# Second attention layer of a four-layer model on one core: where the output bias is added, when the normalised rows are turned, and how VectorE's row work is cut

## The reference, cut to what matters

```python
q = (query @ Wq + bq).reshape(b, sq, 16, 64)      # query = layernorm(x), without gain or bias
k = (ctx @ Wk + bk).reshape(b, 154, 16, 64)
v = (ctx @ Wv + bv).reshape(b, 154, 16, 64)
attn = softmax(einsum('bqhd,bkhd->bhqk', q, k) / 8)
out = einsum('bhqk,bkhd->bqhd', attn, v).reshape(b, sq, 1024)
out = out @ Wo + bo + residual                    # residual = query
y = layernorm(out) * ln_gamma + ln_beta
x = x + tanh(g_xattn[1]) * y
```

## Time and profile before

| what | us |
| --- | --- |
| median of 3 runs | 1551.88 (1550.76 to 1552.78) |
| the profiled execution, its own time | 1550.85 |
| its span in the profile | 1548.9 |
| of it, the 32 units of layer 1's attention, first exponential to last output bias product | 314.4 to 569.1 |
| PE busy over the whole span | 1357.6 (88%) |
| DVE, ACT, POOL busy | 944.2, 723.3, 529.6 |

### The profile page before, as it was taken

How to read it: one execution, slowest core, us unless ns; L and a number is a source line. 1 busy time by engine, 2 the same in 40 slices (tenths; PEclk the granted TensorE clock), 3 DMA queues, 4 the chain that set the end, 5 groups by cost and what they waited for, 6 DMA issues and landing times. The chain is left out here.

```text
span 1548.9 us, 25635 instructions
## 1 busy us (share of the span) xinstructions
PE 1357.6 (88%) x9124; PEld 767.6 (50%) x9124; DVE 944.2 (61%) x2135; ACT 723.3 (47%) x1950; POOL 529.6 (34%) x625
## 2 busy tenths in 40 slices
PE   5899779879989989987998889899987988998998
PEld 3544337545555646554433556565654444443443
DVE  6566621454656664267664888878774855665764
ACT  3355413466656434343443565656664243453222
POOL 2410340545333262342001474747552220001443
PEclk9799989999999999998999999999988997999999
DMA  2445120201000012322120000000000001000000
GB/s 62 138 131 131 42 68 26 44 7 15 1 1 1 1 38 72 95 67 55 35 52 1 1 1 1 1 1 1 2 1 0 1 14 20 10 2 1 7 7 14
DMA packets 66992, 45.31 MB, mean 29 GB/s; under 512 B 17564, under 2 KB 60261, under 8 KB 66869
## 3 DMA queue, kind: packets, MB, share of 16 engines
q1 hardware_dynamic: 61013, 34.48, 8.7%
q0 software_dynamic: 4096, 8.40, 2.1%
q10 hardware_dynamic: 1760, 0.82, 0.3%
HBM read 24.91 MB, written 13.89 MB: 25 GB/s over the span
## 5 line engine op out<-in xcount | busy, mean ns | idle before, releaser
L3464 ACT ACTIVATE L2a_pr<-psum,L2a_negmax 128x512 f32<-128x512 f32 (+3 forms) x256 | 132.0, 530 | 94.3 <-DVE L2a_negmax L3590 40.2
L573 ACT ACTIVATE L1x_praw<-psum,L1x_negmax 128x154 f32<-128x154 f32 x256 | 95.9, 391 | 81.4 <-DVE L1x_negmax L669 81.2
L318 POOL TENSOR_TENSOR L1x_pm<-L1x_praw,L1x_total 128x1024 f32<-128x1024 f32 x32 | 60.7, 1898 | 145.2 <-DVE L1x_total L675 90.4
L84 PE MATMUL psum<-ident 128*128 128x512 f32 x178 | 93.4, 664 | 16.3 <-PEq L3875 7.5
L3326 PE MATMUL psum<-ident,L2a_pr 128*128 128x128 f32 x640 | 85.9, 278 | 19.2 <-DVE L2a_pT L3603 11.9
L669 DVE TENSOR_REDUCE L1x_negmax<-psum 128x4 f32<-128x616 f32 x64 | 50.8, 795 | 57.7 <-PE psum L370 57.0
L3326 PEld LDWEIGHTS psum<-ident,L2a_pr 128*128 128x128 f32 x640 | 71.7, 142 | 25.0 <-issue 21.3
L2016 POOL TENSOR_TENSOR L3f_scaled<-L3f_sg,L3f_wide 128x512 f32<-128x512 f32 (+1 forms) x44 | 55.7, 1271 | 66.4 <-ACT L3f_sg L2097 43.9
L1649 DVE TENSOR_REDUCE L3x_negmax<-psum 128x6 f32<-128x924 f32 (+1 forms) x48 | 47.8, 1012 | 43.9 <-PE psum L1181 35.5
L3212 POOL TENSOR_TENSOR L2a_pr<-L2a_pr,L2a_total 128x768 f32<-128x768 f32 x32 | 48.7, 1520 | 69.9 <-DVE L2a_total L3619 69.6
L3209 POOL TENSOR_TENSOR L2a_pr<-L2a_pr,L2a_total 128x1024 f32<-128x1024 f32 x29 | 56.5, 1949 | 46.1 <-DVE L2a_total L3619 46.0
(11 more groups left out here) (745 smaller groups left out, 3423.1 us busy)
## 6 DMA issues: line engine op xcount, KB each, us to landing
expert_arena<-in_L_ffn_w SPq DMA_DIRECT2D x16, 256.0 KB, 4.4
group_in<-zero SPq DMA_DIRECT2D x2, 1472.0 KB, 9.6
L1f_xs<-group_in SPq DMA_DIRECT2D x10, 256.0 KB, 4.1
group_out<-L1f_ys SPq DMA_DIRECT2D x10, 256.0 KB, 2.3
L1f_gu<-in_L_ffn_gate_up_w SPq DMA_DIRECT2D x8, 256.0 KB, 3.3
slots_in<-zero SPq DMA_DIRECT2D x1, 1280.0 KB, 10.4
L0f_xs<-slots_in SPq DMA_DIRECT2D x5, 256.0 KB, 4.0
resid<-in_x SPq DMA_DIRECT2D x4, 256.0 KB, 5.7
```

Of the source, the lines that this page charges most:

```text
L84: self.nc.tensor.matmul(self.psum[:, bank, :].rearrange("p (t d) -> p t d", d=D), self.ident[:], self.ident[:].unsqueeze(1).to_broadcast([ ...
L318: nc.gpsimd.tensor_tensor(pm[:, n % 2].rearrange("p j t k -> p (j t) k"), praw[:, n % 3, :, :, 0:MAIN].rearrange("p j t k -> p (j t) k"), ...
L573: nc.scalar.activation(praw[:, n % 3, j, t, :], psum[:, 2 * u + j, x * CTX:(x + 1) * CTX], ACT.Exp, bias=negmax[:, n % 2, u, j, x:x + 1], ...
L3464: ins = nc.scalar.activation(pr[:, i % RING, SEQ * j + lo:SEQ * j + hi], psum[:, bank + j, lo:hi], ACT.Exp, bias=negmax[:, i % RING, e:e + ...
```

## The change: what it does

1. **Bias.** The L421 products go. Before the loop one product of ones with `bo` gives all 128 partitions the bias (`bob`), and GpSimd adds it to the normalised rows `xn` of the batch, in place, after its work on unit 2, 10, 18 and 26. `finished`'s first step waits for this (`biased`).
2. **Output between the turned tails and their copy.** TensorE's `output(n-5)` moves ahead of the two waits and of whatever stood in H1, right behind `tails`.
3. **Turned rows a unit ahead.** Batches 2 and 3 have their rows turned at the end of units 7 and 15 in bank H1, and not in units 8 and 16 in H0; `turned` of units 8 and 16 waits for ScalarE's copy of them (`xt`). In unit 0 ScalarE's copy of batch 1's turned rows goes between the two halves of the exponentials. `normed(2)` and `normed(3)` move to units 6 and 14.
4. **ScalarE's square roots.** `rows_root` moves to units 5 and 13, `root` stays at g = 6 (units 14, 22, 30); both now stand between `exps(n, 0)` and `exps(n, 1)`.
5. **VectorE's row work in parts.** `summed` is cut in three and `finished` in six; parts now stand between the copies of the turned weights and `maxima(n, 1)` (units 3, 11, 12, 14, 15, 16, 22, 23, 24, 30, 31, 32) or at the end of the body.

```diff
@@ gpsimd
+                    if n % NG == 2:
+                        f = n // NG
+                        pool.wait_ge(s["xt_ps"], f + 1)
+                        rows_b = xn[:, f % 3]
+                        nc.gpsimd.tensor_tensor(rows_b, rows_b, bob[:].unsqueeze(1).to_broadcast([P, QT, D]), ALU.add).then_inc(s["biased"], 1)
@@ tensor, output(m)
-                                                start=(g == 0 and t == 0), stop=False, skip_group_check=True)
-                    if g == NG - 1:
-                        if b == 0:
-                            pe.wait_ge(s["bo"], 1)
-                        for t in range(QT):
-                            last = nc.tensor.matmul(psum[:, OUT, t * P:(t + 1) * P], core.ones[0:1, :], bo[0:1, :],
-                                                    start=False, stop=True, skip_group_check=True)
+                                                start=(g == 0 and t == 0), stop=(g == NG - 1), skip_group_check=True)
@@ tensor, before the loop
+                    if i == 3:
+                        pe.wait_ge(s["bo"], 1)
+                        nc.tensor.matmul(psum[:, OUT, 0:D], core.ones[0:1, :], bo[0:1, :], start=True, stop=True).then_inc(s["bob_ps"], 1)
@@ tensor, the loop
+                            if b in (1, 2) and g == 0:
+                                pe.wait_ge(s["xt"], b + 2)
...
-                            if g == 0:
-                                rowsT(b + 1, H0)
+                            if n == 0:
+                                rowsT(1, H0)
                             query(n + NG, H0)
...
                     if n >= 3 and n % 2 and n - 2 < NS:
                         tails(n - 2)
+                    if 0 <= n - 5 < NS:
+                        output(n - 5)
                     if n < NS:
                         if n >= 2:
                             pe.wait_ge(s["pt"], 2 * (n - 2) + 2)
...
+                        if b < 2 and g == 7:
+                            rowsT(b + 2, H1)
...
-                    if 0 <= n - 5 < NS:
-                        output(n - 5)
@@ scalar, the loop
                         exps(n, 0)
+                        if n == 0:
+                            rowsT(1, H0)
+                        if n in (5, 13):
+                            rows_root(2 + n // NG)
+                        if g == 6 and b:
+                            root(b - 1)
                         exps(n, 1)
...
-                        if g == 0:
-                            rowsT(b + 1, H0)
                         query(n + NG, H0)
+                        if b < 2 and g == 7:
+                            rowsT(b + 2, H1)
...
-                    if n == 6:
-                        rows_root(2)
-                    if g == 6 and b:
-                        if b == 1:
-                            rows_root(3)
-                        root(b - 1)
@@ vector, before the loop
                     value(1, i, i)
+                    if i == 0:
+                        dve.wait_ge(s["bob_ps"], 1)
+                        nc.vector.tensor_copy(bob[:], psum[:, OUT, 0:D]).then_inc(s["bob"], 1)
@@ vector, the loop (behind turned(n - 2), ahead of maxima(n, 1))
+                    if n == 3:
+                        summed(2, 1)
+                    if n == 11:
+                        summed(3, 0)
+                    if n == 12:
+                        summed(3, 2)
+                    if b:
+                        if g in (6, 7):
+                            finished(b - 1, g - 5)
+                    if b >= 2 and g == 0:
+                        finished(b - 2, 4)
                     if n < NS:
                         maxima(n, 1)
@@ vector, the loop (end of the body)
+                    if n == 2:
+                        summed(2, 0)
+                    if n == 3:
+                        summed(2, 2)
+                    if n == 6:
+                        normed(2)
+                    if n == 11:
+                        summed(3, 1)
+                    if n == 14:
+                        normed(3)
                     if b and g == 5:
                         finished(b - 1, 0)
...
+                    if b and g == 7:
+                        finished(b - 1, 3)
                     if b >= 2 and g == 0:
-                        finished(b - 2, 2)
+                        finished(b - 2, 5)
```

More of the change, by code:

```diff
@@ L255, in wide_attention @@
         "bq", "pad", "vec", "xn", "xt_ps", "xt", "q_ps", "q", "k_ps", "k", "v_ps", "v", "v_act", "sc", "mx", "ex", "rs", "nm", "nt",
-        "tr", "pt", "tt_ps", "tt", "pv", "o", "op", "yr", "yvar", "ysd", "bo_ps", "bo", "rvar", "rsd", "summed")}
+        "tr", "pt", "tt_ps", "tt", "pv", "o", "op", "yr", "yvar", "ysd", "bo_ps", "bo", "rvar", "rsd", "summed", "bob_ps", "bob", "biased")}
     back = [nc.alloc_semaphore(f"{L}_back{b}") for b in range(B)]
@@ L629, in _, with summed @@
                 v = Steps(dve, s["vec"], 0, 0)
-                def summed(b):
-                    dve.wait_ge(back[b], 16 * 2 * QT)
-                    pairs = results[b].rearrange("p (k d) -> p k d", d=D)
-                    wt = core.slot_wt[:, b * QT:(b + 1) * QT, :].rearrange("p t r -> p (t r)")
-                    v.step(nc.vector.tensor_tensor(pairs, pairs, wt.unsqueeze(2).to_broadcast([P, 2 * QT, D]), ALU.mult))
-                    v.done()
-                    halves = results[b].rearrange("p (t r d) -> p t r d", r=2, d=D)
-                    nc.vector.tensor_tensor(y[:], halves[:, :, 0, :], halves[:, :, 1, :], ALU.add).then_inc(s["summed"], 1)
-                    dve.wait_ge(s["summed"], b + 1)
-                    update_rows(core, v, b, y[:].rearrange("p t d -> p (t d)"), slots_gate, y, parts, mv)
-                    nc.vector.tensor_scalar(core.std[:, b * QT:(b + 1) * QT], core.stat[:, b * QT:(b + 1) * QT, 1], LN_EPS, None, ALU.add).then_inc(s["rvar"], 1)
+                def summed(b, part):
+                    rows_b = y[:].rearrange("p t d -> p (t d)")
+                    if part == 0:
+                        dve.wait_ge(back[b], 16 * 2 * QT)
+                        pairs = results[b].rearrange("p (k d) -> p k d", d=D)
+                        wt = core.slot_wt[:, b * QT:(b + 1) * QT, :].rearrange("p t r -> p (t r)")
+                        v.step(nc.vector.tensor_tensor(pairs, pairs, wt.unsqueeze(2).to_broadcast([P, 2 * QT, D]), ALU.mult))
+                    if part == 1:
+                        v.done()
+                        halves = results[b].rearrange("p (t r d) -> p t r d", r=2, d=D)
+                        nc.vector.tensor_tensor(y[:], halves[:, :, 0, :], halves[:, :, 1, :], ALU.add).then_inc(s["summed"], 1)
+                        dve.wait_ge(s["summed"], b + 1)
+                        add_rows(core, v, b, rows_b, slots_gate, y)
+                    if part == 2:
+                        keep_rows(core, v, b, y, parts, mv)
+                        nc.vector.tensor_scalar(core.std[:, b * QT:(b + 1) * QT], core.stat[:, b * QT:(b + 1) * QT, 1], LN_EPS, None, ALU.add).then_inc(s["rvar"], 1)
                 def normed(b):
@@ L691, in finished @@
                         dve.wait_ge(s["op"], NG * (b + 1))
+                        dve.wait_ge(s["biased"], b + 1)
                         nc.vector.tensor_tensor(y[:], psum[:, OUT, :].rearrange("p (t d) -> p t d", d=D), xn[:, b % 3], ALU.add).then_inc(s["yr"], 1)
@@ L700, in finished @@
                         nc.vector.tensor_scalar(sdv[:], mv[:, :, 1], LN_EPS, None, ALU.add).then_inc(s["yvar"], 1)
-                    if part == 1:
+                    if part == 2:
                         dve.wait_ge(s["ysd"], b + 1)
@@ L706, in finished @@
                             v.step(nc.vector.tensor_scalar(y[:, t, :], y[:, t, :], mv[:, t, 0:1], sdv[:, t:t + 1], ALU.subtract, ALU.mult))
+                    if part == 3:
                         v.done()
@@ L721, in _ @@
                     value(1, i, i)
-                summed(0)
+                    if i == 0:
+                        dve.wait_ge(s["bob_ps"], 1)
+                        nc.vector.tensor_copy(bob[:], psum[:, OUT, 0:D]).then_inc(s["bob"], 1)
+                for part in range(3):
+                    summed(0, part)
                 normed(0)
-                summed(1)
+                for part in range(3):
+                    summed(1, part)
                 normed(1)
@@ L768, in _ @@
                             grouped.table(dve, v, 0)
-                finished(B - 1, 0)
-                finished(B - 1, 1)
-                finished(B - 1, 2)
+                for part in range(6):
+                    finished(B - 1, part)
 def add_rows(core, v, b, src, gate, new, base=None):
```

16 lines of the change are left out of this document (4 added, 12 removed).

## The result

The changed kernel takes 1541.64 us in the median of 12 runs (1536.02 to 1546.6), the kernel before, on the same chip, 1552.33 (1548.61 to 1562.0, 12 runs). The medians differ by 10.7 us. The ratio of the two kernels' runs is 0.9921, 95% interval 0.9905 to 0.9937: 12 us less, 10 to 15. The forecast was 1542.2, in the range 1536 to 1549, and faster at 0.86.

A forecast was written before the change was run, and what follows sets the result against it. The prediction took TensorE's own list to bound the middle of the stage. Gains of 17.3 us less losses of 7.7 gave 9.6: 1541.2 us for the profiled run, 1542.2 against the median, range 1536 to 1549.

The forecast's parts named there:

- Output ahead of the waits: TensorE's output product moved ahead of the copy waits: mostly 0.83 us a unit, unit 21 losing 0.6; 7.3 us won.
- Bias: Four bias products of 1.08 us leave TensorE's loop, 4.3 us, less 0.3 ahead of the loop: 4.0 us won.
- Turned rows: Rows turned a unit ahead: 3.17 us won in unit 16 and 1.3 in unit 8, 4.5 in all.
- First units: Units 0 to 5: earlier rows copy and spread sums put TensorE 1.0 us ahead in unit 5.
- Unit 12: Sums leave the front of the maxima, ending the projection's 0.4 us wait for turned copies: 0.5 us won.
- Square roots: ScalarE's roots between the exponentials' halves delay query copies in units 5, 14, 22 and sums in 30: 3.6 us lost.
- VectorE's parts: Row work ahead of the second maxima, slowed beside GpSimd's product, stalls units 11, 12, 15, 16, 23: 4.1 us lost.
- Rival A: Cover is better: TensorE never catches up with the late copies, losses vanish, 17.3 us won: 1534.6 us; 14%.
- Rival B: VectorE's parts pay for all three GpSimd products, and for its bias in unit 11: 4 us more, 1546 us; 13%.
- Rival C: No change: parts and roots cost what was won around them, or gaps reappear at the 1.47 waits: 1551 us; 9%.
- Rival D: Slower: new stalls halve TensorE's clock, 1.7 us a drop; six drops use up the 9.6, ten make 1559 us; 5%.
- a sign of being wrong: In TensorE's clock: a halved clock in stretches that were at 1.0 before would show the prediction wrong.

The follow-up runs named there:

- the fastest kernel: Changed kernel with square roots behind the query copies, sums in three parts behind the second maxima, OUT read a unit earlier; ratio to before 0.9824.
- the kernel with roots and parts back: Changed kernel with square roots behind the query copies and VectorE's row work whole behind the second maxima again; ratio to before 0.9913.
- the sums spread: Changed kernel with square roots behind the query copies and the row sums in three parts, each behind second maxima; ratio to before 0.9865.
- the two experiments: Kernel before with only the rows turned a unit ahead, ratio 0.9960; fastest kernel with rows turned in units 8 and 16 again, ratio to before 0.9899.
- the kernel with the roots back: Changed kernel with only ScalarE's square roots behind the query copies again, VectorE's parts still ahead of the second maxima; ratio to before 0.9899.
- OUT read earlier: Kernel with spread sums and square roots behind the query copies, OUT read in units 12, 20, 28, not 13, 21, 29; ratio to before 0.9824.

## Why the prediction was right

The time, the sign and the mechanism came out: gross gain against stalls behind late query copies. Its net for the stage was 9.9 (9.6 and the 0.3 ahead of the loop); measured are 12.4. That the median, 1541.6, lies only 0.6 from the forecast's 1542.2 is partly luck: by the ratio, the 1551.88 that it started from become 1539.6, which is 2.6 lower, about what the stage won beyond the forecast. Step by step:

- **Output ahead of the waits, 7.3.** From the starts of unit after unit in the traces, units 5, 7, 9, 11, 15, 17 and 19 win 1.05 to 1.07 each and not 0.83, 7.4 in all; units 23 and 27 win 0.8 and 0.9, unit 25 nothing; unit 21 loses 1.0, and 0.15, 0.4, 0.15, 0.14 and 0.76 come back as short waits in units 20, 18, 22, 24 and 26. With 0.3 at the end the sum is 6.8; the ninth wait of 0.83, in unit 31, wasn't in the forecast's list. Both the single gain and what is given back had been set too low.
- **Bias, 4.0.** 4.3 in the stage (shown by its removal from the fastest kernel), less 0.5 ahead of the loop. GpSimd's additions cost nothing, as said. Not seen: the products of unit 12 had been cover worth 1.25. It was cover for what VectorE's sums in one piece delay: the same 1.25 stands in the kernel with roots and parts back, and with the sums spread no turning behind unit 12 waits.
- **Turned rows, 4.5.** 3.7 to 4.9 in the two experiments; the waits of the earlier trace rows and of the earlier trace rows for `L1x_xnT` are gone.
- **First units, 1.0.** 2.2, with a scatter of 1 or more. The 3.64 of the earlier trace rows shrank to 2.16, as worked out, and unit 4's second scores come 2.1 earlier (1.9 was said). The forecast then let half of it be lost again by unit 5; it was not. (By its two rows `summed(2)` takes 4.7 us and not 4.8; no term hangs on that.)
- **Unit 12, 0.5.** 0.9, in the kernels where no part stands ahead of its maxima.
- **Square roots, 3.6.** 3.6 by undoing them. The places were less well met than their sum: unit 5 cost 1.3 (forecast 0.2, on the ground that its scores are late against the exponentials; in the trace they are late by 0.13 alone, 347.01 against 346.88; and the odd unit's list, 5.94 in the forecast, is 5.71), unit 14 1.6, of which 0.4 comes back in unit 15 and is lost again in unit 16, unit 22 0.1 to 0.5 (1.0), unit 30 0.7 (0.5), unit 13 nothing, as said.
- **VectorE's parts, 4.1.** 2.6 from unit 5 on, against pieces behind the maxima: 0.87 in unit 11, 1.15 in unit 12, 0.7 in units 14 to 16, 0.3 in 23 and 0.3 near the end, against 0.8 won back in unit 25, where TensorE then doesn't wait for the turned weights' copy. This is the term that was mis-sized, in units 11, 12 and 16 and by the gain that it had not.

So the losses were 6.2 and not 7.7, and the first units gave 1.2 more: with these two the stage's 9.9 becomes 12.6, against 12.4 measured. The errors of the output term (0.5 too high) and of unit 12 (0.4 too low) nearly cancel. Rival A (no losses) falls by the kernel with the roots back, and again by the one with the sums spread. Rival B falls: L644 was held by one product of GpSimd and not by three. Rival C would have needed losses of 17.3, where 6.2 were measured. Rival D: the halved clock takes 10.24 us of the stage, before and after; one stretch of 3.4 moved from 521 to 339 us, behind a pause of 1.59 in unit 4, and no stretch was added. This row (columns as in the result) is of a stretch that stood at 1.0 before. The prediction had named that as a sign of being wrong, but with 10.24 us of half clock in both it costs the stage nothing.

```profile
339.30:342.70 3.40, 3.40 (x19) 2.03 (x17) 2.65 (x5) 1.66 (x9) 2.54 (x3) 0.51 0.00 0
```

What none of the steps had: the row sums in one piece would have cost 1.43 + 1.25 us in unit 12 once output and bias were gone. The parts ahead of the maxima were better than that and worse than parts behind.

Two rules had been weighed. By the Trainium skill ("SBUF — State Buffer", "Who interferes with whom") the later of two such operations is blocked for the whole of the earlier. L644 began 0.91 before GpSimd's product ended; blocked fully it would take 0.91 + 1.22 = 2.13, and it took 1.98. The gated addition of unit 16, begun 0.90 before the end, took 1.45 where the rule gives 0.90 + 0.75 = 1.65. The trace nearly agrees: both are 0.15 to 0.2 us shorter. The forecast's start at 2.05 behind the unit's start gave an end of 3.27 where 3.13 was measured. By the Trainium skill ("ScalarE: Activation LUTs", "What ACT_TABLE_LOAD costs") each switch costs the load and as much again. Here the load is 1.28, what follows starts 0.02 later, and all roots together cost 3.6 and not 3.6 + 11.6. The advice in the Trainium skill ("ScalarE: Activation LUTs", "Table sets: the hidden batching unit") is to do all the exponentials together and then all the square roots. Here it is the place that counts: behind the query copy the same loads cost TensorE next to nothing (in the kernel with the roots back the turning behind unit 14 waits 0.19), between the halves they cost the 3.6.

## What to carry to other kernels

Before work is put inside a chain, measure from starts how long the bottleneck's own list is until it needs the chain's result; only what exceeds that costs, and it differs from unit to unit (0.6 and 1.1 us here). A product that is taken off the bottleneck may have been the cover of a late copy, and a wait removed shows the next late engine, so the worth of an edit read alone (4.5 and 3.3 us) can be half or three quarters of its worth in company (8.8 and 4.3). Short pieces of another engine's background work belong behind the urgent instruction, one to a unit, and not ahead of it: that, the square roots behind the copies and an earlier read of one bank won another 9.9 us over the changed kernel, from unit 5 on.

## What the runs showed of the hardware

The idle time in the profile's brackets undercounts a pause of TensorE, because the ends of pipelined products are modelled: ahead of the output product 0.83 was shown and 1.06 won, and 1.47 shown and 1.70 won (unit 13, OUT read earlier); ahead of the turning 1.34 was shown and 1.41 lost. A bracket can also name the wrong one of two copies that an engine waits for, as in unit 23 above. And a VectorE product of two SBUF operands (128x1024) takes 1.22 us alone and 1.98 when begun halfway into GpSimd's 1.9 us product; the gated addition 0.75 alone and 1.45 in units 16 and 24, each time begun 1.0 us into that product:

```profile
428.01 1.45 DVE L810 SCALAR_TENSOR_TENSOR L1x_y<-L1x_y,gate,resid 128x512 f32<-128x512 f32 x1
```
